# Second and third of four chained attentions: softmax sums beside PV, one reciprocal for eight heads, units in another order

## The chip, the core and the metric

One core of one Trainium2 chip runs the whole program. The metric is the device time of one execution in microseconds (us), from the host's start of the program to its end. TensorE is called PE here, VectorE DVE, ScalarE ACT, GpSimd POOL, and SyncE, which issues the transfers, SP.

## What is computed

Four cross-attentions in a chain, for 8 batches. Each takes the result of the one before as its queries (or latents) and a context of 256 columns or 128 rows as its keys. All have 16 heads. The second and third, which the change is about, are these (128 queries; 256 keys in the second, 128 in the third; 16 numbers per head):

```python
# second (L1): h = the context's 128 rows and then the 128 latents x
q  = (x @ q_w + q_b).reshape(b, 128, 16, 16)
k, v = split(h @ kv_w + kv_b)                  # 256 keys
attn = softmax(mask(q k^T / 16))
x1 = rmsnorm(attn v @ out_w + out_b + x, w)
x  = gelu(x1 @ mlp_w1 + mlp_b1) @ mlp_w2 + mlp_b2 + x

# third (L2): y = layer_norm(x), keys from the context's 128 rows
attn = softmax(mask(q k^T / 4))
h = attn v @ cproj_w + cproj_b + x
x = h + gelu(layer_norm(h) @ fc_w + fc_b) @ proj_w + proj_b
```

The first attention (L0) has 16 heads of 64 numbers with 256 queries and 256 keys, then an output projection and a layer norm. The fourth (L3) has 8 numbers per head, and takes the mean and the standard deviation of the values under the softmax.

## The kernel before

**Stages.** For each batch b the program works through L1, its MLP, L2, its MLP and L3. The L0 of batch b + 1 is laid between these pieces, and so are the projections of batch b + 1 (`qp0` to `qp3`, `kp0` to `kp3`, `vp0` to `vp3`: queries, keys and values), which fill gaps on PE. A last part, `mixed`, runs the second half of L0 for batch b + 1 and the whole of L3 for batch b step by step, in the order of the table `BOTH`. Batch 7 has no next batch, so L3 stands alone there (`LAST3`).

**Softmax in two passes.** For every group of heads a first pass in bf16 computes scores into the PSUM banks `MX` (a unit 0 or 2: two banks each), DVE takes their negated maxima with `tensor_reduce` (L1358) into `nm`, PE transposes these (a unit "T") and DVE copies them to `nmT` (L1345). The second pass computes the scores in f32 into the banks `SC`, with the maxima added by a matmul, and ACT takes the exponential into one of four slots of `Pr`. A group in L1 and L2 is 8 heads, in two halves of the partitions: two maxima units and a "T".

**PV in L1 and L2** (L886). The values of a head are 32 columns wide: 16 values and 16 ones. So one matmul gives the weighted values and, in the other 16 rows, the sum of the exponentials. Four heads (a quarter g) lie below each other in one PSUM bank. There are two PV banks, so the quarters g = 2 and 3 wait until DVE has finished g = 0 and 1. For each quarter DVE runs `quotient`: a gate instruction, a shuffle that lays the sums on the rows of the values (L1422), a reciprocal (L1423) and a product into `Ax` (L1424). The output projection `slots_out` (L948) has one matmul per quarter, four in all, since half of the rows are padding.

**What sets the order.** Nothing is scheduled at run time. Each engine works through its own list in the order of the code, with semaphores between the engines: `MX_SEQ` and `PV_SEQ` say which bank each use takes, in turns of two, and the outputs of projections take the two `GP` banks in turn, in the order of the list `BODY`. In L1 the order on PE is: maxima of group 0, transposed latents and the second value projection (`amid1`), `qp0`, "T", maxima of group 1 between the score steps, PV one step behind the scores, with `qp1`, `vp0` and the first maxima of the next L0 between. In L2 it is the same with `vp3` and one L0 unit, and then `k3` (L1046, keys of L3), the first two matmuls of the output, an L0 "T" with its scores, and the last two. DVE empties the `GP` banks of `qp0` to `qp3` into `Q0` (L1332); ACT empties those of `kp` and `vp`.

**Before L3** the three units `ENTRY` (first group's maxima and "T") run right ahead of L3's first scores, after L0's score step 4 and its PV.

Of the kernel before, what the change touches and what calls it, by code (L numbers as in the profile page):

```python
# [63 lines left out]
def alone(L):  # L64
# [14 lines left out]
LAST3[0][3].insert(0, (3, 1, 0))  # L79

# [5 lines left out]
def sequences():  # L86
# [9 lines left out]
    def mix(b, start, stop):  # L96
        for L, k, middle, end in mix_of(b)[start:stop]:
            if (L, k) == (3, 0):
                units(b, ENTRY)
# [11 lines left out]
    for b in range(B):  # L111
        more = b < B - 1
        banks0(b, [("xT",), ("lat",)] + [(1, g) for g in range(NG)])
# [6 lines left out]
        banks0(b, [(2, g) for g in range(NG)])  # L120
# [25 lines left out]
V_STEPS = 2 + 8 * 2 + 4  # L146
# [24 lines left out]
def build(nc, z_in, ctxT_in, ctx_in, mask1, mask2, mask3, w0, wo, w1qk, w1v, w1o, w1a, w1b,  # L171
          w2qkv, w2o, w2a, w2b, w3, cols_in, rows_in, ident_in, hmask_in, sel_in, out):
    with ExitStack() as stack:
# [21 lines left out]
        W1O = sb("W1O", [P, NG, D])  # L195
        W2QKV = sb("W2QKV", [P, 3, 2, D])
        W2O = sb("W2O", [P, NG, D])
# [10 lines left out]
        sums2 = sb("sums2", [P, 2, 32])  # L208
        stat0 = sb("stat0", [P, 20])
# [37 lines left out]
        V1 = sb("V1", [P, 2, NH, 32])  # L247
        K2 = sb("K2", [P, 2, P])
        K2b = sb("K2b", [P, 2, P], BF16)
        V2 = sb("V2", [P, NH, 32])  # L250
        K3 = sb("K3", [P, 2, D])
        K3b = sb("K3b", [P, 2, D], BF16)
        V3 = V1
        Ax = sb("Ax", [P, NG, P])
        junk3 = Ax[:, 0:2, :].rearrange("p g k -> p (g k)")
# [27 lines left out]
        scratch = nc.dram_tensor("scratch", [P, NG, D], F32, kind="Internal").ap()  # L283

# [106 lines left out]
        def pv_bank_taken(*use):  # L391
# [11 lines left out]
            return s_Ax, 8 * b + 4 * (kind - 1) + which[0] + 1  # L403
# [145 lines left out]
        def _(pe):  # L549
# [244 lines left out]
            def mixed(b, steps, make):  # L794
# [11 lines left out]
                for i in steps:  # L806
                    L, k, middle, end = mix[i]
                    if (L, k) == (3, 0):
                        for name in ENTRY:
                            unit(*name)  # L810
# [43 lines left out]
            def attention12(b, L, make, K, V, v_ready, amid=lambda: None, after=lambda i: None):  # L854
# [36 lines left out]
                entry, then = (UNITS1[:4], [UNITS1[4:5], UNITS1[5:]]) if L == 1 else (UNITS2[:3], [UNITS2[3:]])  # L891
                for _, g, u in entry:
                    if (g, u) == (0, "T"):
                        amid()
                    make(g, u)
                steps = [(c, kc) for c in range(2) for kc in range(halves)]
                for i, (c, kc) in enumerate(steps):
                    scores(c, kc)
                    if i == 1:
                        pe.wait_ge(*v_ready)  # L900
                    for _, g, u in (then[i] if i < len(then) else []):
# [9 lines left out]
            def body(b):  # L911
# [30 lines left out]
                def slots_out(name, W, which, between=None):  # L942
# [879 lines left out]
```

## Time and profile before

| | |
|---|---|
| median of 3 executions | 1221.82 us (1220.92 to 1226.72) |
| the profiled execution's own time | 1221.06 us |
| its span | 1219.3 us |
| PE busy | 991.2 us, 81% |
| DVE busy | 615.7 us, 50% |
| ACT busy | 463.1 us, 38% |
| POOL busy | 267.1 us, 22% |
| mean granted PE clock | 0.947 of full speed |

The span runs from the first to the last instruction, and the time of the execution lies 1.8 us above it. The first 71.8 us are the prologue (loads of the weights, projections and L0 of batch 0). From there on the batches follow each other at a nearly constant distance: the first DVE instruction of a batch (L1500) starts at 71.80, 212.85, 355.88, 499.25, 642.71, 785.99, 929.75 and 1072.68 us. The rows below are from the third of them, which is typical for the six in the middle. In a timeline row "[1.29 <-DVE Ax L1424]" means that the engine sat idle for 1.29 us before the row, and that the DVE instruction of line 1424, which writes `Ax`, released it. An f32 matmul shows as two records, so "x16" on L886 are 8 matmuls. PE works pipelined: the time from the start of one row to the start of the next says what a row costs in a stream, and the duration in the second column is longer.

### The profile page before, as it was taken

The page shows a single profiled execution, that of the slowest core. Times are in us where ns is not written, and L with a number is a line of the kernel's source. Part 1 is how long each engine was busy: PE and PEld are TensorE (multiplying, and loading weights), DVE is VectorE, ACT ScalarE, POOL GpSimd, SP SyncE. Part 2 cuts the span into 40 slices and gives each one's busy share as a digit, 9 for nine tenths or more (in the row PEclk, how much of TensorE's full clock was granted, in tenths as well). Part 3 has the DMA queues.
Part 4 walks back from the last instruction along what each step waited for, and adds up shares of the span by engine and source line. Part 5 has one row for each costly group of instructions (what it writes and reads, how often), then busy time and mean ns, then how long its engine had stood idle before and what let it go on. Part 6 is the DMA issues. An engine that isn't in the chain of part 4 may idle for free.

```text
span 1219.3 us, 20340 instructions
## 1 busy us (share of the span) xinstructions
PE 991.2 (81%) x7888; PEld 612.9 (50%) x7888; DVE 615.7 (50%) x1263; ACT 463.1 (38%) x881; POOL 267.1 (22%) x386
## 2 busy tenths in 40 slices
PE   7888789897897878888798878979788887976672
PEld 6465444564454654555546644546535454444430
DVE  1444544555546654465455555465544555554431
ACT  1414244343442444344342424424343344422223
POOL 0311111142111510232111421115112231023103
PEclk9899999999999999999999999999989999998667
DMA  9200120010200111002200102001020012001001
GB/s 379 93 1 1 70 95 26 6 70 5 96 31 1 74 51 55 22 2 74 95 19 14 66 10 95 31 2 74 9 87 31 2 74 86 17 16 69 5 1 35
DMA packets 29054, 60.60 MB, mean 50 GB/s; under 512 B 9376, under 2 KB 21024, under 8 KB 24096
## 3 DMA queue, kind: packets, MB, share of 16 engines
q1 hardware_dynamic: 28960, 59.29, 13.3%
q8 instruction: 65, 1.06, 0.4%
q14 instruction: 29, 0.24, 0.1%
HBM read 54.04 MB, written 5.24 MB: 49 GB/s over the span
## 4 chain that ended last, share of the span: by engine, by line
PE 68%; DVE 21%; issue 7%; ACT 2%; POOL 1%; DMA 1%; DVEq 0%; SPq 0%; POOLq 0%; ACTq 0%
DVE nm L1358 7%; PE GP L956 5%; PE PV L702 5%; PE GP L564 5%; PE GP L965 5%; PE GP L566 5%; DVE U L1423 5%; PE SC L685 3%; PE SC L771 3%; PE GP L938 3%; PE GP L749 3%; PE GP L788 3%; PE SC L873 2%; PE MX L618 2%; PE GP L948 2%
## 5 line engine op out<-in xcount | busy, mean ns | idle before, releaser
L1358 DVE TENSOR_REDUCE nm<-MX 128x2 bf16<-128x512 f32 (+1 forms) x352 | 227.1, 689 | 203.1 <-PE MX L624 111.5
L1672 POOL TENSOR_TENSOR Psum<-Pr 128x512 f32<-128x512 f32 x56 | 70.9, 1266 | 294.4 <-ACT Pr L1164 294.4
L1166 ACT ACTIVATE Pr<-SC,bcol 128x512 f32<-128x512 f32 x128 | 81.1, 684 | 131.5 <-PE SC L771 131.5
L564 PE MATMUL GP<-zP,W 128*128 128x128 f32 x512 | 103.2, 284 | 6.9 <-DMA W<-w 6.9
L1191 ACT ACTIVATE Pr<-SC,bcol 128x512 f32<-128x512 f32 x96 | 60.8, 684 | 115.8 <-PE SC L873 115.8
L566 PE MATMUL GP<-uP,W 128*128 128x128 f32 x512 | 100.1, 277 | 0.0
L1164 ACT ACTIVATE Pr<-SC 128x512 f32<-128x512 f32 x128 | 69.3, 593 | 62.8 <-PE SC L685 62.8
L564 PEld LDWEIGHTS GP<-zP,W 128*128 128x128 f32 x512 | 79.8, 194 | 15.8 <-issue 13.6
L1646 POOL TENSOR_TENSOR stat<-stat,half 128x1 f32<-128x1 f32 x24 | 13.6, 565 | 326.9 <-DVE stat L1532 179.2
L566 PEld LDWEIGHTS GP<-uP,W 128*128 128x128 f32 x512 | 78.9, 195 | 0.0
L702 PE MATMUL PV<-Pr,V 128*64 128x256 f32 x512 | 75.6, 420 | 0.0
L965 PE MATMUL GP<-WB,work 128*128 128x256 f32 x256 | 62.2, 398 | 10.5 <-DVE work L1461 10.5
L771 PE MATMUL SC<-work,K 64*128 64x512 f32 x256 | 70.3, 619 | 0.0
L685 PE MATMUL SC<-Q,K 64*128 64x256 f32 x512 | 70.2, 384 | 0.0
L956 PE MATMUL GP<-oT,WA 128*128 128x128 f32 x512 | 65.2, 289 | 0.9 <-issue 0.8
L956 PEld LDWEIGHTS GP<-oT,WA 128*128 128x128 f32 x512 | 62.4, 203 | 4.8 <-issue 3.5
L886 PE MATMUL PV<-Pr,V 128*32 128x128 f32 x768 | 35.8, 290 | 33.0 <-DVE Ax L1424 32.0
L1423 DVE RECIPROCAL U<-U 128x128 f32<-128x128 f32 x64 | 61.0, 953 | 2.2
L965 PEld LDWEIGHTS GP<-WB,work 128*128 128x128 f32 x256 | 49.4, 198 | 23.2 <-issue 16.5
L1345 DVE COPY nmT<-MX 128x256 bf16<-128x256 bf16 (+1 forms) x96 | 25.7, 267 | 59.4 <-PE MX L657 47.6
L873 PE MATMUL SC<-work,K 64*128 64x512 f32 x192 | 54.8, 638 | 0.0
L685 PEld LDWEIGHTS SC<-Q,K 64*128 64x128 f32 x512 | 51.4, 192 | 4.1
(184 smaller groups left out, 1709.0 us busy)
## 6 DMA issues: line engine op xcount, KB each, us to landing
WA<-w1a SPq DMA_DIRECT2D x8, 1024.0 KB, 6.0
WB<-w1b SPq DMA_DIRECT2D x8, 1024.0 KB, 8.1
WA<-w2a SPq DMA_DIRECT2D x8, 1024.0 KB, 5.0
WB<-w2b SPq DMA_DIRECT2D x8, 1024.0 KB, 7.1
W<-w SPq DMA_DIRECT2D x6, 1024.0 KB, 9.9
scratch<-U SPq DMA_DIRECT2D x16, 256.0 KB, 2.0
C<-scratch SPq DMA_DIRECT2D x96, 32.0 KB
zP<-z_in SPq DMA_DIRECT2D x8, 128.0 KB, 4.3
```

Of the source, the lines that this page charges most:

```text
L564: pe.matmul(dst, W0[:, piece, 2 * s, at:at + P], zP[:, s * P:s * P + P], start=True, stop=False)
L566: mm = pe.matmul(dst, W0[:, piece, 2 * s + 1, at:at + P], uP[:, s * P:s * P + P], start=False, stop=True)
L685: mm = pe.matmul(SC[r][:, kc * D:kc * D + D], K0[half, k, kc * P:kc * P + P], Q0[half, k, :], start=False, stop=True, skip_group_check=True)
L702: mm = pe.matmul(bank[64 * j:64 * j + 64, i * D:i * D + D], V0[:, kc, h * 64:h * 64 + 64], Pr[:, (n + j) % 4, kc * D:kc * D + D], start=(k ...
L771: pe.matmul(SC[j][:].rearrange("p (t l) -> p t l", l=D), K3[half, g % 2, kc * P:kc * P + P], Q3[half, g // 2 * 2:g // 2 * 2 + 2, :], start ...
L873: pe.matmul(SC[r][:].rearrange("p (t l) -> p t l", l=P), K[half, c, kc * P:kc * P + P], Q12[half, 4 * c:4 * c + 4, :], start=False, stop=True,
L956: mm = pe.matmul(g[:, j * P:j * P + P], WA[:, c, f * P:f * P + P], oT[:, c, :], start=(c == 0), stop=(c == 1), skip_group_check=True)
L965: mm = pe.matmul(g[:, 0:D], G[:, f * P:f * P + P], WB[:, f, :], start=(f == 0), stop=(f == 7))
L1166: act.activation(Pr[:, (n + j) % 4, :], SC[j], ACT.Exp, bias=bcol[:, 3 + k % 2:4 + k % 2], scale=8.0 ** -0.5).then_inc(p_ready, 1)
L1358: dve.tensor_reduce(dst, MX[(n + i) % 2][:].rearrange("p (a k) -> p a k", a=a), AX_X, ALU.max, negate=True).then_inc(mx_done, 1)
L1423: chain.step(dve.reciprocal(den, den))
L1672: pool.tensor_tensor(Psum[:, c % 4, :].rearrange("p (a l) -> p a l", l=D), two[:, :, 0:D], two[:, :, D:2 * D], ALU.add)\
```

## The change

It has four parts.

1. **Sums beside PV.** The values are now laid out so that the 32 columns of a head hold 16 values in the lower half for one quarter and in the upper half for the other, with zeros in the rest. Both quarters of a group accumulate into one bank, columns 0 to 127. A second set of matmuls with a small tile of ones (`ones2`) as weights puts the sums at the same rows, columns 128 to 255. `quotient` then needs no shuffle and runs once for 8 heads, twice in a layer in place of four times, with its reciprocal straight from PSUM. `slots_out` has two matmuls. V3 becomes a tile of its own.
2. **Steps in another order in L1 and L2.** The latents' transposes and the second value projection follow the first maxima unit, `qp0` the second; `vp0` moves behind PV; `k3` moves between the score steps of L2; the L0 "T" stands between the two PV steps, and its scores ahead of the two output matmuls.
3. **The entry of L3.** In batches 0 to 6 the three units that begin L3 are spread over L0's score steps 4 and 5 (`BOTH`); step 5 of L0 comes ahead of L3's first scores. The reciprocal of L0's first sums (`reciprocals0`) keeps its place behind the "T" of L3's second group.
4. **Query projections.** `qp0` to `qp3` of the next batch are emptied by ACT, two activations of 256 columns each with a bias, in place of one DVE instruction of 512.

```diff
@@ order of steps, all engines
-        (0, 4, [], []), (3, 0, [], [(3, 1, 0)]), (3, 1, [], [(3, 1, 2)]), (0, 5, [(3, 1, "T")], [(0, 3, 0)]),
-        (3, 2, [], [(0, 3, 2)]), (3, 3, [(0, 3, "T")], [(3, 2, 0)]), (0, 6, [], [(3, 2, 2)]),
+        (0, 4, [(3, 0, 0)], [(3, 0, 2)]), (0, 5, [(3, 0, "T")], [(3, 1, 0)]), (3, 0, [], [(3, 1, 2)]),
+        (3, 1, [(3, 1, "T")], [(0, 3, 0)]), (3, 2, [], [(0, 3, 2)]), (3, 3, [(0, 3, "T")], [(3, 2, 0)]),
...
+def entry(b):
+    return ENTRY if b == B - 1 else []
@@ PE, PV of L1 and L2
                     for r in range(2):
-                        g = 2 * c + r
-                        bank = pv_bank(b, L, g)
                         pe.wait_ge(p_ready, n + r + 1)
-                        if kc == 0:
-                            pe.wait_ge(*pv_bank_taken(b, L, g))
-                        for t in range(4):
-                            mm = pe.matmul(bank[32 * t:32 * t + 32, 0:P], V(HG * g + t, kc),
-                                           Pr[:, (n + r) % 4, t * P:t * P + P], start=(kc == 0),
-                                           stop=(kc == halves - 1), skip_group_check=True)
+                        for at, weights in ((0, lambda t: V(2 * c + r, t, kc)), (P, lambda t: ones2[:, r, :])):
+                            for t in range(4):
+                                mm = pe.matmul(bank[32 * t:32 * t + 32, at:at + P], weights(t),
+                                               Pr[:, (n + r) % 4, t * P:t * P + P], start=(at == kc == r == 0),
+                                               stop=(kc == halves - 1 and r == 1), skip_group_check=True)
@@ PE, slots_out
-                    for s in range(NG):
-                        if s == 2 and between:
-                            between()
-                        pe.wait_ge(s_Ax, 8 * b + 4 * which + s + 1)
+                    for s in range(2):
+                        pe.wait_ge(s_Ax, 4 * b + 2 * which + s + 1)
@@ PE, L1
-                def amid1():
+                def amid1(g, u):
+                    if (g, u) == (0, 0):
...
+                        v1("v1c", 0)
+                    if (g, u) == (0, 2):
+                        fill("qp0")
...
-                    if i in (1, 2):
-                        fill("qp1" if i == 1 else "vp0")
+                    if i == 1:
+                        fill("qp1")
...
+                fill("vp0")
                 slots_out("o1", W1O, 0)
@@ PE, L2
+                def before2(i):
+                    if i == 0:
+                        g, full = begin("k3", (ld_w3, 16))
...
                 def after2(i):
-                    if more and i == 0:
-                        make03[0](1, 2)
+                    if more:
+                        make03[0](1, "T" if i else 2)
...
-                def between2():
-                    if more:
-                        make03[0](1, "T")
-                        scores0(b + 1, 2)
-                slots_out("o2", W2O, 1, between2)
+                if more:
+                    scores0(b + 1, 2)
+                slots_out("o2", W2O, 1)
@@ ACT
+                if name[0] == "q":
+                    for c in range(2):
+                        ins = act.activation(Q0[:, 2 * i + c, :], g[:, c * D:c * D + D], ACT.Identity,
+                                             bias=col("rwb", 2 * i + c))
+                    ins.then_inc(s_Q0, 1)
...
-                attention12(b, 1, 1.0 / 16, lambda i: cast(b + 1, 0) if more and i == 3 else None)
+                fill("qp0")
+
+                def after1(i):
+                    if more and i == 3:
+                        fill("qp1")
+                        cast(b + 1, 0)
+                attention12(b, 1, 1.0 / 16, after1)
...
-                fill("vp2", "vp3")
-                attention12(b, 2, 0.25)
-                g = take(o, "k3")
+                fill("qp2", "vp2", "vp3")
+
+                def keys3(i):
+                    if i != 1:
+                        return
+                    g = take(o, "k3")
...
+                attention12(b, 2, 0.25, keys3)
...
+                fill("qp3")
                 turned("yT2", "ln2w", "ln2b")
@@ DVE
-                    if L == 0 and k == 5:
+                    if (L, k) == ((0, 5) if b < 0 else (3, 1)) and b < B - 1:
                         reciprocals0(b + 1, 0)
...
-            def quotient(b, L, g):
+            def quotient(b, L, m):
...
-                chain.step(dve.stream_shuffle(den, bank, [16 + r % 16 for r in range(32)]))
-                chain.step(dve.reciprocal(den, den))
-                dve.tensor_tensor(Ax[:, g, :], bank, den, ALU.mult).then_inc(s_Ax, 1)
+                chain.step(dve.reciprocal(den, bank[:, P:2 * P]))
+                dve.tensor_tensor(Ax[:, m, :], bank[:, 0:P], den, ALU.mult).then_inc(s_Ax, 1)
```

**PE, end of L2, before**: L886 is PV (all four quarters), L1046 is `k3`, L948 the output, L657 the L0 "T", L679 and L685 its scores.

```order
L660 MATMUL MX<-identb,nm 128x128
L603 MATMUL MX<-K0b,Qb 128x256 x4
L869 MATMUL SC<-nmT,sel 128x128 x8
L873 MATMUL SC<-work,K 128x512 x2
L886 MATMUL PV<-Pr,V 32x128 x16
L1046 MATMUL GP<-uC,W 128x256
L948 MATMUL GP<-W2O,Ax 128x256 x2
L657 MATMUL MX<-identb,nm 128x128 x2
L679 MATMUL SC<-nmT,sel 128x512 x2
L685 MATMUL SC<-Q,K 128x256 x4
L948 MATMUL GP<-W2O,Ax 128x256 x2
L702 MATMUL PV<-Pr,V 64x256 x4
```

The same place after; L897 is PV with its sums, L667 the L0 "T", L689 and L695 its scores, L958 the output.

```order
L897 MATMUL PV<-Pr,V 32x128 x4
L897 MATMUL PV<-Pr,ones 32x128 x4
L897 MATMUL PV<-Pr,V 32x128 x4
L897 MATMUL PV<-Pr,ones 32x128 x4
L667 MATMUL MX<-identb,nm 128x128 x2
L897 MATMUL PV<-Pr,V 32x128 x4
L897 MATMUL PV<-Pr,ones 32x128 x4
L897 MATMUL PV<-Pr,V 32x128 x4
L897 MATMUL PV<-Pr,ones 32x128 x4
L689 MATMUL SC<-nmT,sel 128x512 x2
L695 MATMUL SC<-Q,K 128x256 x4
L958 MATMUL GP<-W2O,Ax 128x256 x2
```

PV has twice the matmuls, the L0 "T" has moved between its two steps, the output's two matmuls stand together behind L0's scores, and `k3` has gone forward (it now stands between the two score steps, ahead of these rows).

**PE, where L3 begins, before**: L679 and L685 are L0's score step 4, L702 its PV, L723 its sums, L618 and L624 the maxima of L3, L657 their "T", L767 and L771 L3's first scores.

```order
L679 MATMUL SC<-nmT,sel 128x512 x2
L685 MATMUL SC<-Q,K 128x256 x4
L702 MATMUL PV<-Pr,V 64x256 x4
L723 MATMUL PV<-Psum,sums 32x256 x4
L618 MATMUL MX<-b3row,sel 128x512 x2
L624 MATMUL MX<-K3b,Q3b 128x256 x4
L618 MATMUL MX<-b3row,sel 128x512 x2
L624 MATMUL MX<-K3b,Q3b 128x256 x4
L657 MATMUL MX<-identb,nm 128x128 x2
L767 MATMUL SC<-nmT,sel 128x256 x4
L771 MATMUL SC<-work,K 128x512 x2
L702 MATMUL PV<-Pr,V 64x256 x4
```

And after, where every line number is 10 higher:

```order
L689 MATMUL SC<-nmT,sel 128x512 x2
L695 MATMUL SC<-Q,K 128x256 x4
L628 MATMUL MX<-b3row,sel 128x512 x2
L634 MATMUL MX<-K3b,Q3b 128x256 x4
L712 MATMUL PV<-Pr,V 64x256 x4
L733 MATMUL PV<-Psum,sums 32x256 x4
L628 MATMUL MX<-b3row,sel 128x512 x2
L634 MATMUL MX<-K3b,Q3b 128x256 x4
L689 MATMUL SC<-nmT,sel 128x512 x2
L695 MATMUL SC<-Q,K 128x256 x4
L667 MATMUL MX<-identb,nm 128x128 x2
L712 MATMUL PV<-Pr,V 64x256 x4
```

Between the first maxima unit and the second now stand PV and sums of L0, and between the second and the "T" L0's score step 5.

**DVE, end of L1, before** (L425 is the gate, L1529 takes the output) and, in the second fence, after (L435 the gate, L1451 and L1452 the quotient, L1393 maxima of the next L0, L1557 takes the output):

```order
L1423 RECIPROCAL U<-U 128x128
L1424 TENSOR_TENSOR Ax<-PV,U 128x128
L1358 TENSOR_REDUCE nm<-MX 128x2 x2
L425 TENSOR_TENSOR gate<-half 128x1
L1422 STREAM_SHUFFLE U<-PV 128x128
L1423 RECIPROCAL U<-U 128x128
L1424 TENSOR_TENSOR Ax<-PV,U 128x128
L425 TENSOR_TENSOR gate<-half 128x1
L1422 STREAM_SHUFFLE U<-PV 128x128
L1423 RECIPROCAL U<-U 128x128
L1424 TENSOR_TENSOR Ax<-PV,U 128x128
L1529 TENSOR_TENSOR xa<-GP,res 128x256
```

```order
L435 TENSOR_TENSOR gate<-half 128x1
L1451 RECIPROCAL U<-PV 128x128
L1452 TENSOR_TENSOR Ax<-PV,U 128x128
L1393 TENSOR_REDUCE nm<-MX 128x2 x4
L435 TENSOR_TENSOR gate<-half 128x1
L1451 RECIPROCAL U<-PV 128x128
L1452 TENSOR_TENSOR Ax<-PV,U 128x128
L1557 TENSOR_TENSOR xa<-GP,res 128x256
```

Four quotients have become two, without shuffles, and both maxima units of the next L0 stand between them.

## Rows read from the trace of the kernel before

**Rows 1.** The page's first part: busy time, share of the span, instructions.
```profile
PE 991.2 (81%) x7888; PEld 612.9 (50%) x7888; DVE 615.7 (50%) x1263; ACT 463.1 (38%) x881; POOL 267.1 (22%) x386
```

**Rows 2.** Waits over the span: waiter, releaser, us in total, times, longest.
```profile
PE PV L886 <- DVE Ax L1424: 32.0, 23, 2.1
...
PE GP L948 <- DVE Ax L1424: 27.4, 30, 1.8
```

**Rows 3.** Windows of batch 2: length, busy times (instructions), granted PE clock, DMA share, GB/s.
```profile
355.90:499.20 143.30, 121.21 (x988) 74.78 (x987) 76.88 (x157) 57.63 (x110) 33.42 (x47) 0.98 0.12 43
419.00:435.40 16.40, 10.72 (x93) 5.89 (x93) 9.44 (x26) 5.82 (x11) 2.39 (x4) 0.90 0.03 10
461.70:480.00 18.30, 17.41 (x152) 8.36 (x152) 9.99 (x16) 8.76 (x15) 2.54 (x2) 0.91 0.05 15
```

**Rows 4.** Timeline of PE in L1: start, duration, line, instruction, idle before and releaser.
```profile
367.14 0.39 PE L638 MATMUL MX<-b1row,sel 64*128 64x512 bf16 x2 [1.56 <-DVE nm L1358]
...
371.77 0.39 PE L638 MATMUL MX<-b1row,sel 64*128 64x512 bf16 x2 [0.95 <-DVE nmT L1345]
...
376.26 0.69 PE L886 MATMUL PV<-Pr,V 128*32 128x128 f32 x16
...
376.88 0.49 PE L564 MATMUL GP<-zP,W 128*128 128x128 f32 x2
...
385.88 0.42 PE L886 MATMUL PV<-Pr,V 128*32 128x128 f32 x8 [1.29 <-DVE Ax L1424]
...
389.71 0.70 PE L948 MATMUL GP<-W1O,Ax 128*128 128x256 f32 x2 [1.45 <-DVE Ax L1424]
391.31 0.70 PE L948 MATMUL GP<-W1O,Ax 128*128 128x256 f32 x2 [0.91 <-DVE Ax L1424]
391.85 0.28 PE L657 MATMUL MX<-identb,nm 128*128 128x128 bf16 x2
```

**Rows 5.** Timeline of PE in L2, to the transposes behind it.
```profile
421.78 0.40 PE L603 MATMUL MX<-K0b,Qb 64*128 64x256 bf16 x4 [0.41 <-DVE nmT L1345]
...
423.31 0.64 PE L886 MATMUL PV<-Pr,V 128*32 128x128 f32 x16
425.70 0.43 PE L886 MATMUL PV<-Pr,V 128*32 128x128 f32 x8 [1.75 <-DVE Ax L1424]
...
431.33 0.39 PE L679 MATMUL SC<-nmT,sel 64*128 64x512 bf16 x2 [0.39 <-DVE nmT L1345]
...
432.93 0.70 PE L948 MATMUL GP<-W2O,Ax 128*128 128x256 f32 x2 [0.35 <-DVE Ax L1424]
...
435.45 1.08 PE L702 MATMUL PV<-Pr,V 128*64 128x256 f32 x8
...
439.78 0.41 PE L930 MATMUL GP<-ident,xb 128*128 128x128 f32 x2 [1.27 <-DVE xb L1472]
```

**Rows 6.** Timeline of PE where L3 begins.
```profile
457.67 0.39 PE L618 MATMUL MX<-b3row,sel 64*128 64x512 bf16 x2 [1.58 <-DVE nm L1358]
...
459.84 0.27 PE L657 MATMUL MX<-identb,nm 128*128 128x128 bf16 x2 [1.56 <-DVE nm L1358]
...
461.71 1.97 PE L702 MATMUL PV<-Pr,V 128*64 128x256 f32 x8
```

**Rows 7.** Groups of instructions: busy us, mean ns of one, idle before them.
```profile
L1358 DVE TENSOR_REDUCE nm<-MX 128x2 bf16<-128x512 f32 x320 | 206.5, 690 | 189.7 <-PE MX L624 111.5 <-PE MX L603 54.0 <-PE MX L644 24.2
...
L1423 DVE RECIPROCAL U<-U 128x128 f32<-128x128 f32 x64 | 61.0, 953 | 2.2
L1191 ACT ACTIVATE Pr<-SC,bcol 128x512 f32<-128x512 f32 x96 | 60.8, 684 | 115.8 <-PE SC L873 115.8
...
L1404 DVE RECIPROCAL xb<-PV 128x256 f32<-128x256 f32 x16 | 28.0, 1753 | 2.3 <-PE PV L720 1.2 <-DVE work L1412 0.5
...
L1424 DVE TENSOR_TENSOR Ax<-PV,U 128x128 f32<-128x128 f32 x64 | 18.7, 292 | 2.2
...
L1256 ACT ACTIVATE K1b<-GP,cols 128x256 bf16<-128x256 f32 x16 | 6.7, 472 | 25.0 <-PE GP L938 25.0
```

More of the change, by code:

```diff
@@ L112, in sequences @@
         more = b < B - 1
-        banks0(b, [("xT",), ("lat",)] + [(1, g) for g in range(NG)])
+        banks0(b, [("xT",), ("lat",), (1, 0), (1, 1)])
         units(b, UNITS1)
@@ L119, in sequences @@
             banks0(b + 1, [("pv", 0)])
-        banks0(b, [(2, g) for g in range(NG)])
+        banks0(b, [(2, 0), (2, 1)])
         units(b, UNITS2)
@@ L808, in mixed @@
                     if (L, k) == (3, 0):
-                        for name in ENTRY:
+                        for name in entry(b):
                             unit(*name)
@@ L852, in mix_end, with attention12 @@
                     project("kp0", order_of(b + 1), b + 2)
[L854 removed]
+            def attention12(b, L, make, K, V, v_ready, amid=lambda g, u: None, before=lambda i: None,
+                            after=lambda i: None):
                 halves = 2 if L == 1 else 1
@@ L898, in attention12 @@
                     scores(c, kc)
+                    before(i)
                     if i == 1:
                         pe.wait_ge(*v_ready)
-                    for _, g, u in (then[i] if i < len(then) else []):
+                    for _, g, u in (units[cuts[i]:cuts[i + 1]] if i + 1 < len(cuts) else []):
                         make(g, u)
@@ L1320, in _ @@
             chain = Chain(dve, v_step, V_STEPS)
-            apart = Apart(dve, gate[:, 1:2], v_apart, 11)
+            apart = Apart(dve, gate[:, 1:2], v_apart, 7)
             def take(o, name):
@@ L1372, in mixed @@
                     if (L, k) == (3, 0):
-                        for name in ENTRY:
+                        for name in entry(b):
                             unit(*name)
@@ L1386, in mix_end, with attention12 @@
                     quotient0(b + 1, 3)
-            def attention12(b, L, amid=lambda: None, after=lambda: None, during=lambda g: None):
-                units = UNITS1 if L == 1 else UNITS2
-                for _, g, u in units:
-                    if (g, u) == (0, "T"):
-                        amid()
+            def attention12(b, L, amid=lambda g, u: None):
+                for _, g, u in UNITS1 if L == 1 else UNITS2:
                     maxima(b, L, g, u)
-                after()
-                for g in range(NG):
-                    quotient(b, L, g)
-                    during(g)
+                    amid(g, u)
             def reciprocals0(b, half):
@@ L1519, in body, with amid1 @@
                 more = not is_last(b)
-                def after1():
-                    fill("qp1")
-                    if not is_first(b):
-                        end3(b - 1)
-                attention12(b, 1, lambda: (v1("v1c", 0), fill("qp0")), after1,
-                            lambda g: maxima(b + 1, 0, 0, 2 * g) if more and g < 2 else None)
+                def amid1(g, u):
+                    if (g, u) == (0, 0):
+                        v1("v1c", 0)
+                attention12(b, 1, amid1)
+                if not is_first(b):
+                    end3(b - 1)
+                quotient(b, 1, 0)
+                if more:
+                    maxima(b + 1, 0, 0, 0)
+                    maxima(b + 1, 0, 0, 2)
+                quotient(b, 1, 1)
                 g = take(o, "o1")
@@ L1549, in body @@
                     maxima(b + 1, 0, 1, 0)
-                fill("qp2")
                 blocks12(b, o, 2)
-                attention12(b, 2, after=lambda: maxima(b + 1, 0, 1, 2) if more else None,
-                            during=lambda g: maxima(b + 1, 0, 1, "T") if more and g == 1 else None)
+                attention12(b, 2)
+                if more:
+                    maxima(b + 1, 0, 1, 2)
+                quotient(b, 2, 0)
+                if more:
+                    maxima(b + 1, 0, 1, "T")
+                quotient(b, 2, 1)
                 g = take(o, "o2")
```

123 lines of the change are left out of this document (65 added, 58 removed), and 4 rows, old and new, of the table BOTH.

## The prediction

> **What bounds the kernel now.** I read the page first: PE is busy for 991 of 1219 us, and no other engine for more than 616 [rows 1]. So PE sets the pace, and the question is only how much of its idle and slow time the change removes and how much work it adds. The list of waits comes next. Two of PE's longest have one releaser, the product at the end of a quotient: 32.0 us before PV of L1 and L2, which wants its bank back, and 27.4 us before the output projections [rows 2]. A window over one batch gives the budget: 143.3 us with PE busy for 121.2 [rows 3], which leaves 22.1 us idle. The clock is a second loss. Over two stretches of that batch it is granted at 0.90 and 0.91 [rows 3], which means 1.2 GHz for 3.3 us of each and 2.4 GHz for the rest, some 1.65 us lost in each. The timelines of PE show where the waits lie; they repeat in all middle batches. I work out one batch, and multiply by 7. The last batch has no work of a next batch to move.
>
> **First attention of the pair (L1).** At its start PE waits 1.56 us for the first maxima and 0.95 us for the copy of their transpose [rows 4], 2.51 in all. The latents' transposes and the second value projection move into the first of these. At 0.54 us per f32 matmul of 256 columns (391.31 to 391.85, [rows 4]) they fill about 1.15 us of it, and 0.4 stay. The copy no longer queues behind the emptying of qp0 on DVE; the wait for such a copy with nothing in front is 0.41 [rows 5]. Gain 2.51 - 0.4 - 0.4 = 1.7 us.
>
> At its end three waits for `Ax` go: 1.29, 1.45 and 0.91 [rows 4], 3.65 us. A wait costs PE more than its idle figure, since the pipeline empties first: I take 0.15 us for each, 0.45. Two of four output matmuls go, 1.08. Against this stands what PV gains in work. 16 records of PV take 0.62 us from their start to that of the next row (376.26 to 376.88, [rows 4]), and a call now has 32. The trace has no call with sums beside it. The least is 0, if the sums ran alongside in other columns; the most is 0.245 us for each of 16 records, a pair of full matmuls being 0.49 [rows 4], 3.9 us. I take the row that is nearest, the same form with the same shapes: 0.62 us more for each call, 2.5 for four.
>
> What is late next is ACT: it now empties qp1 (two activations at 0.47, [rows 7]) and makes the two casts for the next L0 before the third pair of exponentials (2 x 0.68), while vp0, which covered that, has moved back. I charge 0.6 us of wait, with 0 and 1.5 as ends. The last quotient has gate, reciprocal 0.95 and product 0.29 [rows 7]. The reciprocal now reads PSUM; the trace has this form only at twice the width, 1.75 us [rows 7], so it costs between 0.95 and 1.75, and I take 0.95, nearly all of its time being per element (1.75 is less than twice 0.95). It starts behind the reduces of the next L0's second unit (2 x 0.69, [rows 7]), and is done about 1.8 us after PV; vp0 covers that. Gain 3.65 + 0.45 + 1.08 - 2.5 - 0.6 = 2.1 us.
>
> **Second attention (L2).** From the L0 unit at 421.78 to the PV of L0 at 435.45 it takes 13.7 us now [rows 5]. I walk through what follows. k3 moves ahead of the "T"; it takes about 1.0 us and covers a wait of 0.4, so the L0 unit starts 0.6 later, and PV at 423.9 in place of 423.31. PV 1.24, the L0 "T" 0.15, PV 1.24: 426.5. None of the two waits for a quotient, since each has a bank of its own. DVE can begin the first quotient at 425.1: gate 0.15, 0.95, 0.29, then the copy of the "T", about as long as the product, with hops 0.2: 427.0, so that L0's scores wait 0.5. They take 1.25 us (431.33 to 432.93 less the wait of 0.35, [rows 5]): 428.35. The second quotient is ready at 428.4. Two output matmuls: 429.4. Gain 435.45 - 429.4 = 6.05 us; it is the largest term, as waits of 1.75, 0.41, 0.39 and 0.35 us ([rows 5], and others between those rows) and the slow clock of this stretch lie in it.
>
> Behind it the transposes of xb come 4.33 us after the output (435.45 to 439.78, [rows 5]), with a wait of 1.27 that the emptying of qp3 on DVE helped to cause. PV of L0 and qp3 need 2.9, plus 0.3 for exponentials that are now late: gain 1.1. But ACT empties qp3 first (0.94) and oT after it, and that holds the MLP up by 0.55. Gain 0.55. In front of L2, qp2 on ACT costs 0.1.
>
> **Entry of L3.** Two waits of 1.58 and 1.56 [rows 6] go with 0.3 for the pipeline, 3.45 us: L0's PV, sums and scores now stand where PE waited for the reduces. What follows at half clock (8 records of L0's PV in 1.97 us, [rows 6], against 1.08, [rows 5]) returns to full speed, 1.65. New waits: a unit's reduces take 1.38 [rows 7] plus two hops, and the work between is a little shorter in three places, 0.15 + 0.35 + 0.35. The move of L0's first reciprocal on DVE (1.75) stays behind the same "T". Gain 4.25 us.
>
> **At nothing:** the four DVE projections that go (DVE is idle half of the time), memsets in the prologue, where all wait for weights, and V3's own tile. SP issues the same transfers in the same order, and none lies in a gap above.
>
> **Sum.** 1.7 + 2.1 + 6.05 + 0.55 - 0.1 + 4.25 = 14.55 us per batch, 101.9 for seven. In the last batch nothing can be moved into the gaps, ACT bounds L1 and the entry of L3 is unchanged; I give it 3 us, a fifth of the others. Together 104.9, against the profiled execution's own 1221.06 us: 1116 us. The median is 0.8 above that execution, within the noise. As a check, a batch would take 128.8 us with PE busy for 121.2 + 6 x 0.62 - 4 x 0.54 - 3.3 = 119.5, 93%.
>
> **Rivals.** (1) The clock stays down in both stretches. For it: the new order still has five short waits there. Against it: every fall in the timeline follows a group of waits that are gone. Price 3.3 x 7 = 23 us: 1139 us. The Trainium skill, "TensorE: Matmul & The Clock Gate", section "A second HAM failure mode: psum-queue depth-cycling", speaks for it: a PE that idles briefly between groups often enough has its clock swing between the levels. Rows show both levels near waits, not which length of wait decides. (2) ACT becomes what PE waits for. Four emptyings of 0.94 stand in its queue ahead of exponentials, casts or oT. I charge 0.6 + 0.55 + 0.1; if all 3.76 come on the path, 2.5 x 7 = 18 us: 1134 us. Against it: ACT is idle in more than half of the batch. (3) The new order hides nothing, as its waits come back one step later: 1.7 + 4.25 less per batch, 42 us: 1158 us. Against it: the work moved in is longer than each wait but three. (4) The slower side: the ones do not run four abreast like the values, but one after another at 0.245 us each. That is 3.3 us more per call, 48 calls, 158 us: 1274 us. It decides from 105 / 48 = 2.2 us over my 0.62, or 0.18 us a record. Against it: values with the same shape take 0.039 us each (0.62 / 16).
>
> **Chances.** Forecast, 1100 to 1130 by itself: 0.62. Rival 1: 0.13. Rival 2: 0.12. Rival 3: 0.07. Rival 4: 0.03. The sums run for nothing (-30 us, 1086): 0.03. The range 1092 to 1150 holds the first three. A measurement can tell 0.5%, 6 us, from no change: faster 0.96, within 0.01, slower 0.03.
>
> **What would show it.** Batches 127 to 131 us apart. No wait of PV in L1 and L2 for DVE, and at most 0.6 us before the output of L2. The call of PV at 1.2 to 1.3 us from start to start: over 2 shows rival 4. Full clock between L2's PV and its output, and at the start of L3: else rival 1. The wait of L1's fourth score step for ACT near 0.6, and the MLP's first matmul about 0.5 later against the transposes: if over 1, rival 2. If the first maxima of L3 still have waits over 1 us behind them, rival 3. The forecast is wrong if the batches are more than 135 us apart.

## The result, and the profile after

The changed kernel takes 1095.26 us (median of 4 runs, 1094.25 to 1096.86) against 1223.36 us for the kernel before, run beside it: a ratio of 0.895, 95% interval 0.893 to 0.898. I had predicted 1116 us, with a range of 1092 to 1150. The direction and the mechanism held; 127.2 us of span went where I had counted 104.9. The page's first line, against [rows 1]:

```profile
PE 955.9 (88%) x8592; PEld 608.2 (56%) x8592; DVE 541.6 (50%) x1012; ACT 484.3 (44%) x937; POOL 268.1 (25%) x389
```

PE is busy for only 35 us less, so most of the gain is idle time. Windows over the third batch (323.44 to the next start), the end of L2 and the entry of L3, with columns as in [rows 3]:

```profile
323.44:449.98 126.54, 117.28 (x1076) 74.77 (x1075) 67.17 (x125) 60.68 (x118) 33.49 (x47) 1.00 0.14 49
381.00:391.30 10.30, 8.98 (x124) 5.25 (x122) 5.79 (x14) 4.94 (x9) 3.16 (x6) 1.00 0.04 14
415.00:433.00 18.00, 16.28 (x158) 7.49 (x154) 10.87 (x18) 7.72 (x13) 1.95 (x2) 1.00 0.10 23
```

A batch takes 126.5 us instead of 143.3, PE's idle time in it falls from 22.1 to 9.3 us, and the clock is full in both stretches that ran at 0.90 and 0.91. The waits on `Ax` of [rows 2], 27.4 and 32.0 us, have shrunk to this, and none of them is before PV any more:

```profile
PE GP L958 <- DVE Ax L1452: 2.1, 3, 0.9
```

To place the gain I read four starts on DVE in each batch: the sum `x0` (batch start), the two sums `xa` behind the outputs of L1 and L2, and `x3` behind the second MLP. The distances in the third batch, in us, with those of the experiments below (the last batch runs from its `x0` to the end of the span):

| kernel | x0 to xa of L1 | to xa of L2 | to x3 | to next x0 | batch | last batch |
|---|---|---|---|---|---|---|
| before | 36.17 | 43.50 | 15.99 | 47.71 | 143.37 | 146.62 |
| changed | 31.45 | 36.57 | 15.22 | 43.33 | 126.57 | 135.43 |
| e1 old entry of L3 | 31.45 | 36.58 | 15.21 | 48.68 | 131.92 | 136.06 |
| e2 queries on DVE | 31.70 | 36.42 | 16.09 | 43.33 | 127.54 | 136.56 |
| e3 old order in L1, L2 | 33.44 | 37.27 | 15.57 | 43.33 | 129.61 | 136.41 |
| e4 layout only | 33.98 | 37.13 | 16.45 | 48.73 | 136.29 | 140.16 |
| e5 ones three times | 32.75 | 37.00 | 15.22 | 43.33 | 128.30 | 138.12 |
| e6 reciprocal twice | 32.78 | 38.21 | 15.03 | 43.33 | 129.35 | 140.77 |
| e7 e1, waits filled | 31.44 | 36.58 | 15.22 | 46.13 | 129.37 | 137.18 |
| e8 last batch filled | 31.45 | 36.58 | 15.21 | 43.34 | 126.58 | 125.13 |
| e9 before, filled | 36.12 | 41.81 | 15.99 | 46.13 | 140.05 | 130.30 |

At full clock the sections repeat to 0.05 us between kernels that do not differ in them, and from batch to batch but for the first and the fifth, so terms of 0.2 us can be read. Where the clock falls they do not repeat. In the kernel before, L2's section takes 42.63 to 43.50 us over the seven full batches, and the third has the longest; in e1 the entry of L3 takes 47.51 to 48.90. So where the clock is in play I give the mean of the seven batches too. From before to changed the means are 4.64, 6.61, 0.78 and 4.46 us, and in the third batch 4.72, 6.93, 0.77 and 4.38. The total cannot be read finely: the start of the first batch moves between 71 and 74 us, in part because the first matmul waits 6.9 to 8.3 us for its weights. One of the four executions of e1 took 2639.64 us; without it the median of e1 is 1129.9 instead of 1130.3.

PE in the changed kernel from the first PV of L2, against [rows 5]:

```profile
386.30 0.43 PE L897 MATMUL PV<-Pr,V 128*32 128x128 f32 x8
386.54 0.40 PE L897 MATMUL PV<-Pr,ones 128*32 128x128 f32 x8
386.76 0.40 PE L897 MATMUL PV<-Pr,V 128*32 128x128 f32 x8
386.98 0.40 PE L897 MATMUL PV<-Pr,ones 128*32 128x128 f32 x8
387.31 0.29 PE L667 MATMUL MX<-identb,nm 128*128 128x128 bf16 x2
387.53 0.43 PE L897 MATMUL PV<-Pr,V 128*32 128x128 f32 x8
...
389.11 0.39 PE L689 MATMUL SC<-nmT,sel 64*128 64x512 bf16 x2 [0.50 <-DVE nmT L1380]
389.34 1.03 PE L695 MATMUL SC<-Q,K 64*128 64x256 f32 x8
390.29 1.13 PE L958 MATMUL GP<-W2O,Ax 128*128 128x256 f32 x4
391.54 1.08 PE L712 MATMUL PV<-Pr,V 128*64 128x256 f32 x8
```

Where PV waited 1.75 us, the "T" and the other PV call now follow without a wait. The one wait left is the 0.50 us that I had expected. The call takes 1.01 us (386.30 to 387.31), not 1.24. And the entry of L3, against [rows 6]:

```profile
413.37 0.27 PE L667 MATMUL MX<-identb,nm 128*128 128x128 bf16 x2 [0.49 <-DVE nm L1393]
413.58 1.08 PE L712 MATMUL PV<-Pr,V 128*64 128x256 f32 x8
...
419.41 0.27 PE L667 MATMUL MX<-identb,nm 128*128 128x128 bf16 x2 [0.50 <-DVE nm L1393]
...
422.97 0.39 PE L613 MATMUL MX<-K0b,Qb 64*128 64x256 bf16 x4 [0.74 <-DVE nm L1393]
```

The eight records of L0's PV take 1.08 us again, where they took 1.97.

### The profile page after: what moved, and what is told of

It is laid out like the page before. It is cut to its first block, busy times and chain, and to the rows that moved or that the text cites. A ratio compares the mean times of both kernels' runs of the same rounds, so it can differ in the third digit from the quotient of the medians.

```text
span 1092.1 us, 21492 instructions
## 1 busy us (share of the span) xinstructions
PE 955.9 (88%) x8592; PEld 608.2 (56%) x8592; DVE 541.6 (50%) x1012; ACT 484.3 (44%) x937; POOL 268.1 (25%) x389
## 4 chain that ended last, share of the span: by engine, by line
PE 72%; DVE 12%; issue 9%; ACT 4%; POOL 1%; DMA 1%; DVEq 0%; ACTq 0%; POOLq 0%; SPq 0%
DVE nm L1393 6%; PE PV L712 6%; PE GP L966 6%; PE GP L574 6%; PE GP L975 5%; PE GP L576 5%; PE SC L695 4%; PE GP L950 4%; PE SC L884 3%; PE GP L759 3%; PE SC L781 3%; PE GP L798 2%; PE GP L581 2%; PE PV L897 2%; PE MX L628 2%
## 5 line engine op out<-in xcount | busy, mean ns | idle before, releaser
L1393 DVE TENSOR_REDUCE nm<-MX 128x2 bf16<-128x512 f32 (+1 forms) x352 | 227.0, 689 | 169.7 <-PE MX L634 79.6
L712 PE MATMUL PV<-Pr,V 128*64 128x256 f32 x512 | 69.4, 392 | 0.8
L695 PE MATMUL SC<-Q,K 64*128 64x256 f32 x512 | 68.6, 382 | 0.0
L975 PE MATMUL GP<-WB,work 128*128 128x256 f32 x256 | 59.3, 384 | 10.5 <-DVE work L1489 10.5
L781 PE MATMUL SC<-work,K 64*128 64x512 f32 x256 | 67.7, 598 | 0.0
L884 PE MATMUL SC<-work,K 64*128 64x512 f32 x192 | 55.0, 637 | 0.0
L695 PEld LDWEIGHTS SC<-Q,K 64*128 64x128 f32 x512 | 50.9, 190 | 4.3
L1671 POOL TENSOR_TENSOR work<-qs,hmask 128x512 f32<-128x512 f32 x32 | 32.6, 1041 | 82.9 <-DVE Q12b L1467 82.9
L1128 ACT ACTIVATE K<-GP 128x512 f32<-128x512 f32 x32 | 19.1, 597 | 76.0 <-PE GP L576 76.0
L1477 DVE TENSOR_TENSOR work<-GP,cols 128x512 f32<-128x512 f32 x32 | 22.1, 691 | 61.1 <-PE GP L966 61.1
```

The costliest lines, as they stand in the source:

```text
L695: mm = pe.matmul(SC[r][:, kc * D:kc * D + D], K0[half, k, kc * P:kc * P + P], Q0[half, k, :], start=False, stop=True, skip_group_check=True)
L712: mm = pe.matmul(bank[64 * j:64 * j + 64, i * D:i * D + D], V0[:, kc, h * 64:h * 64 + 64], Pr[:, (n + j) % 4, kc * D:kc * D + D], start=(k ...
L781: pe.matmul(SC[j][:].rearrange("p (t l) -> p t l", l=D), K3[half, g % 2, kc * P:kc * P + P], Q3[half, g // 2 * 2:g // 2 * 2 + 2, :], start ...
L884: pe.matmul(SC[r][:].rearrange("p (t l) -> p t l", l=P), K[half, c, kc * P:kc * P + P], Q12[half, 4 * c:4 * c + 4, :], start=False, stop=True,
L975: mm = pe.matmul(g[:, 0:D], G[:, f * P:f * P + P], WB[:, f, :], start=(f == 0), stop=(f == 7))
L1393: dve.tensor_reduce(dst, MX[(n + i) % 2][:].rearrange("p (a k) -> p a k", a=a), AX_X, ALU.max, negate=True).then_inc(mx_done, 1)
```

## The experiments

**e1: the old entry of L3.**

```diff
 def entry(b):
-    return ENTRY if b == B - 1 else []
+    return ENTRY
 # and BOTH, with the place of reciprocals0, as before
```

> The changed kernel with the entry of L3 as before: the three units of maxima in one row ahead of L3's first scores, and the order of the mixed part of L0 and L3 with the place of L0's first reciprocal as before. All else as changed. My theory, by the section from x3 to the next batch's start (47.71 us before, 43.33 after): two waits of about 1.6 us on the reduces and about 1.65 us of half clock come back in each of 7 batches, 4.4 x 7 = 31 us: 1126 us, and a granted clock of about 0.9 at the entry. Rival A: only the waits count and the clock stays at 2.4 GHz since the stretches ahead are denser: 2.7 x 7 = 19 us, 1114 us. Rival B: the section became shorter for another reason (Q3 or the MLP): within 5 us of the changed kernel.

1130.3 us (0.9226 of before, interval 0.9203 to 0.9249). My theory holds: only the last section changes, by 5.35 us in the third batch and 4.82 in the mean of seven, where the change had gained 4.38 and 4.46. The order and the waits are again those of before, but in this batch PE runs at half clock for longer, from the scores at 426.37 on:

```profile
425.61 0.37 PE L667 MATMUL MX<-identb,nm 128*128 128x128 bf16 x2 [1.56 <-DVE nm L1393]
426.37 0.60 PE L777 MATMUL SC<-nmT,sel 64*128 64x256 bf16 x4 [0.39 <-DVE nmT L1380]
426.77 1.91 PE L781 MATMUL SC<-work,K 64*128 64x512 f32 x4
428.61 1.97 PE L712 MATMUL PV<-Pr,V 128*64 128x256 f32 x8
430.52 0.61 PE L628 MATMUL MX<-b3row,sel 64*128 64x512 bf16 x2
```

The matmuls at L781 take 1.91 us here; at full clock they take 1.02 (e7, below).

It is not so in every batch. Windows over 18 us from `x3` on, of the third and the fourth batch:

```profile
417.31:435.31 18.00, 13.94 (x98) 5.99 (x96) 7.08 (x13) 6.92 (x14) 1.99 (x2) 0.81 0.46 160
549.24:567.24 18.00, 13.86 (x114) 6.20 (x114) 7.79 (x15) 7.93 (x15) 2.01 (x3) 0.91 0.46 160
```

Both have the waits of 1.58 and 1.56 us, but the second of them has half the time at 1.2 GHz. The section takes 48.5 to 48.9 us in the first, third, fifth and seventh batch, and 47.5 to 47.6 in the three others.

**e2: queries back on DVE.** `project("qp0")` to `("qp3")` are emptied by one DVE operation each, where they were before.

> The changed kernel with the emptying of the four query projections back on DVE, one operation each, at the places that they had before. My theory: ACT's part costs 1.25 us per batch by the prediction (0.6 + 0.55 + 0.1), and on DVE the copy of the first transpose and xb wait longer again, 0.95 + 0.5 us: the two nearly cancel, 0 to +5 us, 1095 to 1100 us. Rival A: ACT's emptyings are what PE now waits for, and the kernel is faster by up to 1.25 x 7 = 9 us, 1086 us. Rival B: DVE's queue was the true cause of the old waits in L1 and L2: slower by over 15 us.

1102.7 us (0.9005, 0.8985 to 0.9025). Emptying by ACT in place of DVE is a gain of about 1 us per batch (0.97 in the third), and the kernel is 2.7 us above my bound of 1100. The table puts 0.87 of it behind L2, where `xb` waits again:

```profile
395.36 1.08 PE L712 MATMUL PV<-Pr,V 128*64 128x256 f32 x8
...
399.62 0.41 PE L942 MATMUL GP<-ident,xb 128*128 128x128 f32 x2 [1.20 <-DVE xb L1497]
```

That is 4.26 us from L0's PV to the transposes, against 2.94 in the changed kernel (391.54 to 394.48). Rival A, a kernel that is faster without the emptyings on ACT, is refuted.

**e3: the old order within L1 and L2**, on the new layout.

```diff
-                    if i == 1:
-                        fill("qp1")
+                    if i in (1, 2):
+                        fill("qp1" if i == 1 else "vp0")
 # latents, v1c and qp0 behind (0, 2); k3 behind L2; the "T" and
 # scores0(b + 1, 2) between the two output matmuls of L2
```

> The changed kernel with PE's order within L1 and L2 as before: latents' transposes, v1c and qp0 after the second unit, vp0 inside L1's steps instead of ahead of the output, k3 after L2, and the 'T' and the scores of L0 between the two matmuls of L2's output. Layout, entry of L3 and the emptying by ACT stay. My theory, from the terms: 1.15 us at L1's start, about 0.9 us that vp0 covers ahead of L1's output, and of L2's 6 us some 1.5 to 2 (0.5 that k3 covered, a wait for the second quotient partly covered, and some half clock): about 3.8 x 7 = 27 us, 1122 us. Rival A: the layout alone made the gain, and the order is worth under 1 us per batch: below 1102 us. Rival B: the orders carry the clock too: over 40 us, above 1135 us.

1121.5 us (0.9161, 0.9135 to 0.9187), as expected, but in part by luck. The order is worth 1.99 us in L1, where I had 2.05, but 0.70 in L2, where I had 1.5 to 2, and 0.35 behind it. Those 3.04 us make 21 in seven batches; the rest is a first batch that starts 1.5 us later and costs 1.7 us more than the others, and a last one that costs 1.0. Without `vp0` to cover it, the second quotient is what L1's output waits for:

```profile
365.44 0.70 PE L960 MATMUL GP<-W1O,Ax 128*128 128x256 f32 x2 [1.10 <-DVE Ax L1451]
```

**e4: the layout only**, with e1, e2 and e3 undone together.

> Of the change only the layout: sums beside PV in columns of their own, one reciprocal for eight heads, two output matmuls. The entry of L3, PE's orders in L1 and L2 and the emptying by DVE are as before. My theory: the parts add, and the layout is the largest, 128 - 31 - 27 - 3 = 67 us of the gain: 1095 + 61 = 1156 us. Rival A: with the old orders the waits on the second quotient come back in place of those on the bank, and the layout alone gives only half of that: about 1190 us. Rival B: the layout is nearly all of it: below 1130 us.

1171.3 us (0.9557, 0.9528 to 0.9587), between my theory and rival A: the layout alone brings 53 of the 128 us. By section the parts nearly add: this kernel's batch is 9.72 us longer than the changed one's, and e1 to e3 give 5.35 + 0.97 + 3.04 = 9.36. Over seven batches it is 67.2 against 63.1 us; 3.3 of these 4.1 us lie at the entry of L3, where this kernel has the long stretch at half clock in six batches and e1 in four. I had undershot since I had put the three parts too low (61 us for 35, 7.5 and 26 measured), and the last batch adds 4.7 us. The layout alone brings 6.37 of L2's 6.93 us (6.05 of 6.61 in the mean), the clock included. From its window over the section between the two `xa`:

```profile
376.34:413.47 37.13, 34.89 (x290) 23.27 (x288) 20.00 (x39) 18.58 (x36) 17.67 (x27) 1.00 0.17 62
```

**e5: the price of a pass beside PV.**

```diff
-                        for at, weights in ((0, ...), (P, lambda t: ones2[:, r, :])):
+                        for at, weights in ((0, ...), (P, lambda t: ones2[:, r, :]),
+                                            (2 * P, lambda t: ones2[:, r, :])):
```

> The changed kernel with a third pass in each PV call of L1 and L2: 8 more matmuls of the ones for each half, into the unused columns 256 to 383 of the bank. What is computed stays the same. This measures the price of a pass that runs beside PV, 16 records per call, 48 calls. My theory, from the timeline of the changed kernel (a call with sums takes 1.02 us, one without took 0.62): 0.40 x 48 = 19 us, 1114 us. Rival A, the prediction's term: 0.62 x 48 = 30 us, 1125 us. Rival B: the pass is hidden where PE waits anyway for the exponentials: below 5 us, under 1100 us.

1110.4 us (0.9082, 0.9062 to 0.9102). Sixteen records more per call cost 0.44 us where nothing hides them:

```profile
347.65 0.43 PE L898 MATMUL PV<-Pr,V 128*32 128x128 f32 x8
347.89 0.62 PE L898 MATMUL PV<-Pr,ones 128*32 128x128 f32 x16
348.33 0.40 PE L898 MATMUL PV<-Pr,V 128*32 128x128 f32 x8
```

Each 8 records take 0.22 us from start to start (347.89 to 348.33 is 0.44 for 16). Of 6 x 0.44 = 2.64 us per batch 1.73 reach the end: 1.30 of the 1.76 us of L1's four calls, and 0.43 of the 0.88 of L2's two. The rest falls into waits. Both the term of the prediction, 0.62, and rival B are refuted.

**e6: the reciprocal of each quotient twice.**

```diff
-                chain.step(dve.reciprocal(den, bank[:, P:2 * P]))
+                for _ in range(2):
+                    chain.step(dve.reciprocal(den, bank[:, P:2 * P]))
 # and V_STEPS, the count of chained DVE steps, 2 + 8 + 4 in place of 2 + 4 + 4
```

> The changed kernel with the reciprocal of each quotient taken twice, the second one overwriting the first with the same numbers: 32 more DVE instructions of about 0.95 us, each waiting for the one before. My theory: at the ends of L1 and L2 the DVE chain is on the path although DVE is idle half of the time. In L2 the first quotient stands ahead of the copy of L0's 'T' and the second ahead of the output, where PE waits 0.41 and 0.50 us now: 2 x 1.05 us. In L1 vp0 covers about 0.5 of 1.05. That makes 2.6 x 7 = 18 us and 4 us in the last batch: 1117 us. Rival: DVE's idle time takes it up: under 5 us, below 1100 us.

1120.6 us (0.9162, 0.9140 to 0.9185): 2.78 us per batch, 2.6 expected, and 5.3 in the last. DVE is idle half of the time, yet its chain at the ends of L1 and L2 is on the path: the wait ahead of L0's scores is 1.49 where it was 0.50.

```profile
399.47 0.39 PE L689 MATMUL SC<-nmT,sel 64*128 64x512 bf16 x2 [1.49 <-DVE nmT L1380]
```

**e7: e1 with PE busy in the two waits at the entry of L3.** A helper issues n matmuls on constants into unused columns of the bank that is taken next:

```diff
+            def warm(b, name, n):
+                o = order_of(b)
+                pe.wait_ge(*o.bank_taken(name))
+                for _ in range(n):
+                    pe.matmul(GP[o.at(name)[0]][:, D:2 * D].rearrange("p (a k) -> p a k", k=P), identb[:],
+                              sel[:, 0:2, :], start=True, stop=True, skip_group_check=True)
```

> The kernel with the old entry of L3 (the one that measured 1130.3 us), with 10 bf16 matmuls of 256 columns on constants, into unused columns of the bank that u0 takes next, behind each of the two units of maxima that PE waits for there. They fill the two waits of 1.58 and 1.56 us and give nothing else. My theory: the section's 5.35 us over the changed kernel are 2.7 us of waits and 2.65 us of half clock (5.3 us at 1.2 GHz); with PE busy in the waits the clock stays at 2.4 GHz and only the waits are left: 1130.3 - 2.65 x 7 = 1112 us. Rival A: the clock falls by something else than these idle stretches, and the time stays at 1130 us or rises. Rival B: waits and clock are one loss and all of it comes back: 1095 us.

1117.5 us (0.9141, 0.9121 to 0.9160). The section falls from 48.68 to 46.13. So 2.55 us of e1's 5.35 are clock and 2.80 waits, as expected for this batch. In the mean of the seven, e1's 4.82 are 2.01 of clock and 2.81 of waits, since three batches of e1 had the short stretch. The total is 5.5 us above my number. In the profiled executions the clock gives back 14.1 us and not the 18.6 that I had multiplied out, the first batch starts 1.7 us later (74.1 us), and the last one is 1.1 us longer. The same stretch:

```profile
421.92 1.27 PE L591 MATMUL GP<-sel,identb 128*128 128x256 bf16 x10
423.55 0.27 PE L675 MATMUL MX<-identb,nm 128*128 128x128 bf16 x2 [0.36 <-DVE nm L1403]
424.21 0.39 PE L785 MATMUL SC<-nmT,sel 64*128 64x256 bf16 x4 [0.39 <-DVE nmT L1390]
424.44 1.02 PE L789 MATMUL SC<-work,K 64*128 64x512 f32 x4
```

**e8: the changed kernel with its last batch filled.** One `warm` of 3 to 24 matmuls in most long waits of the last batch, as `if not more: warm(b, "yT", 24)` ahead of the transposes of `xb`.

> The changed kernel, with PE kept busy in the last batch: behind most of its waits of over 0.5 us stand 3 to 24 bf16 matmuls of 256 columns on constants, into unused columns of the bank that is taken next, sized to be a little shorter than the wait. My theory: the last batch runs a third of its time at 1.2 GHz (granted 0.83, 0.82, 0.89, 0.77 by section), and PE's own work there lies on the path, so some 8 us come back: 1087 us, with a granted clock of 0.95 or more in the last batch. Rival A: the chain of DVE, ACT and POOL sets the last batch's time, and the clock gives under 2 us. Rival B: the fillers delay the work behind them, since they take longer than the waits: slower than 1095 us.

1085.6 us (0.8879, 0.8861 to 0.8898): the fastest version here. The last batch falls from 135.4 to 125.1 us. The windows over it, of the changed kernel and then of e8:

```profile
956.67:1092.10 135.43, 79.51 (x662) 48.34 (x662) 50.52 (x101) 41.48 (x78) 30.85 (x51) 0.81 0.07 26
```

```profile
956.97:1082.10 125.13, 92.09 (x877) 60.97 (x877) 51.54 (x101) 41.56 (x78) 31.00 (x51) 0.93 0.08 29
```

PE has 215 more matmul records and yet the batch ends 10.3 us sooner: its own work runs at 2.4 GHz to its end. The granted clock is 1.00 until 1065.2 us, and PE's last matmul ends at 1061.6.

**e9: the kernel before with its waits filled**, by the same helper.

> The kernel before, with bf16 matmuls of 256 columns on constants in its longest waits, and nothing else changed: in every batch 12 and 8 of them ahead of the third and fourth quarter of L2's PV, 8 ahead of the last output matmul of L2, 11 and 11 behind the first two units at the entry of L3; in the last batch also in the waits of the kernel whose last batch was filled before. It parts the clock from the waits. My theory: in the two stretches that ran at 0.90 and 0.91, 1.65 us each come back and the waits stay: 3.3 x 7 = 23 us; the last batch (146.6 us) keeps its waits on the quotients but loses its half clock: with the changed kernel's filled last batch at 125.1 us it ends at 129 us, 17 us less. Together 1223 - 40 = 1183 us. So of the change's 11.2 us in the last batch some 7 would be the clock. Rival A: the clock is not held by such filling while the waits are this long: above 1210 us. Rival B: the clock sets most of L2's gain: L2's section falls by 3 us or more from its 43.5, below 1170 us.

1188.6 us (0.9704, 0.9678 to 0.9731), 5.6 above my theory, which holds against both rivals. In the third batch L2's section loses 1.69 us and the last one 1.58: the half clock of [rows 3] and nothing else. At the entry of L3 the clock stays full in all seven batches (1.69 us in the mean). Ahead of it it does not: four batches still have some half clock in L1 or L2. The fourth has it in both, here from `x0` to the first `xa` and on to the second:

```profile
493.85:530.83 36.98, 30.14 (x268) 20.62 (x266) 21.84 (x53) 10.33 (x19) 4.18 (x5) 0.96 0.02 6
530.83:573.75 42.92, 40.51 (x292) 26.62 (x292) 22.95 (x52) 19.90 (x38) 17.07 (x27) 0.95 0.14 53
```

So L2 gives back 1.22 us in the mean, L1 loses 0.44, and the seven batches give 17.3 us where I had 23, which is about what was missing. In the last batch 16.3 us come back:

```profile
1056.90:1187.20 130.30, 94.29 (x806) 61.33 (x806) 58.90 (x129) 41.71 (x78) 31.07 (x51) 0.93 0.08 28
```

At equal clock the last batches differ by 130.30 - 125.13 = 5.2 us.

## Why the prediction held, and which terms were off

**L1: 3.8 forecast, 4.72 measured.** The waits went as said, and ACT's new one is 0.35 us, not 0.6:

```profile
348.43 0.39 PE L880 MATMUL SC<-nmT,sel 64*128 64x128 bf16 x7 [0.35 <-ACT Pr L1215]
```

The mis-sized term is the PV call: I charged 0.62 us for the sums, since 16 records stood 0.62 us from the next row in [rows 4]. Those 0.62 hold something that a call pays once: in the changed kernel each 8 records take 0.22 us, and a call of 32 takes 1.01. The extra is 0.40, and e5 gives 0.44 for the next 16. Four calls at 0.22 us less are 0.9, of which 0.65 would reach the end by the share that e5 measured in L1. With ACT's 0.25 the sum comes to 4.7 to 4.9, against 4.72.

**L2: 5.95 forecast (6.05 less the 0.1 of `qp2`), 6.93 measured.** Two calls explain up to 0.44 more. `k3`, charged at 1.0 us from a stretch at half clock, takes 0.54 (383.65 to 384.19), another 0.46:

```profile
383.65 0.70 PE L1061 MATMUL GP<-uC,W 128*128 128x256 f32 x2
384.19 0.22 PE L670 MATMUL MX<-identb,nm 128*128 128x128 bf16 x1
```

With both my walk gives 6.85. (One of its steps is added up wrong: 427.0 + 1.25 is 428.25 and not 428.35, which moves the end by 0.1 us at most.) e9 shows that 1.69 of the term is clock in this batch, as I had read from the granted 0.90 (1.22 in the mean), and e4 that the layout, not the order, brings nearly all of it. e6 shows that the DVE chain still sets this end.

**Behind L2: 0.55 forecast, 0.77 measured.** The transposes come 1.32 us sooner with `qp3` off DVE (2.94 in place of 4.26), and the MLP's first matmul 0.44 later behind them (1.80 us in place of 1.36): 0.88 against e2, and against my 1.1 - 0.55.

```profile
394.48 0.41 PE L942 MATMUL GP<-ident,xb 128*128 128x128 f32 x2
...
395.53 0.71 PE L1080 MATMUL GP<-W,uC 128*128 128x128 f32 x4 [0.32 <-ACT Q L1124]
396.28 3.81 PE L966 MATMUL GP<-oT,WA 128*128 128x128 f32 x32
```

**Entry of L3: 4.25 forecast, 4.38 measured.** The waits are worth 2.80 (46.13 less 43.33, both at full clock), where I had 3.45 - 0.85 = 2.6. The clock is worth 1.58, where I had 1.65.

**Last batch: 3 forecast, 11.2 measured.** This is the step that failed by most. I said that nothing could be moved there, and scaled the waits. But both last batches have long stretches at half clock, and the change shortens those too: e8 and e9 leave 5.2 us of waits and work, so 6.0 us were clock. The profile of the kernel before shows it in a window over that batch, with a granted clock of 0.76, which my term leaves out:

```profile
1072.68:1219.30 146.62, 86.26 (x574) 51.90 (x574) 57.91 (x129) 41.60 (x78) 30.41 (x51) 0.76 0.07 24
```

Together: the seven full batches gained 115.4 us against 101.9 (of the 13.5 over, the PV calls are at most 6 x 0.22 x 7 = 9.2 and `k3` 3.2), the last one 8.2 more than said, the start of the first batch 0.65. The misses do not cancel, they add: every section of the third batch gained more than forecast, and 126.6 us from batch to batch lies just under the 127 to 131 that I had named. The measured 1095 us is inside the range, but 3 us from its lower end and below the 1100 to 1130 to which I had given 0.62. The other signs came as said: no wait of PV for DVE in L1 and L2, full clock in both stretches, no wait over 1 us at the entry of L3.

**The rivals.** (1) The clock stays down: no; it is 1.00 through the middle batches, with waits of 0.3 to 0.9 us left. The Trainium skill, "TensorE: Matmul & The Clock Gate", section "A second HAM failure mode: psum-queue depth-cycling", spoke for it: it tells of a PE whose short idles between groups of matmuls make the clock swing. This trace does not bear that out for its short waits, behind which the clock is 1.00. Behind two waits of about 1.6 us at the entry of L3 it fell in all seven batches of e1, and with them filled it stayed at 1.00 in all seven (e7). (2) ACT as the bound: no (e2). (3) Waits that only move: no, except for 0.49, 0.50 and 0.74 us at the entry. (4) Ones one after another: no, 0.027 us a record (e5).

## What to carry over

A wait of PE costs its idle time and then, behind some groups of long ones, half clock in the work that follows. The rows do not say which groups: the two of 1.6 us at the entry of L3 did it in every batch, while the three of 1.29, 1.45 and 0.91 us at the end of L1 [rows 4] stand in a window of the kernel before with the full clock:

```profile
384.00:396.00 12.00, 7.88 (x65) 4.03 (x63) 7.15 (x22) 3.49 (x9) 2.24 (x8) 1.00 0.01 1
```

Read the granted clock over every stretch and in every batch, the last one too, and price the two apart: constant matmuls in the waits do it in one run (not in every batch of e9), and where the waits cannot go they are worth keeping (e8). Do not multiply one batch's loss by seven before you have seen that it repeats. A short burst of records timed to the next row holds a cost that a longer burst pays only once; take the price of more records from the distance between rows inside a burst. An engine that is idle half of the time can still end the path, so lengthen its chain once to see.

## What the runs showed that I had not expected

The same waits in the same order cost a different amount of clock, and this in one and the same kernel. Behind 1.58 and 1.56 us at the entry of L3 the section of e1 is longer than that of e7, which has the full clock, by 1.4 us in three batches and by 2.4 to 2.6 in four. The kernel before has the small loss in six batches, 1.58 us in the third (e9), and the large one in the sixth, where the section takes 48.45 us and not 47.7; e4 has the small loss in its first batch (47.78) and the large one in the others. The sixth batch of the kernel before, in a window of 18 us from `x3` on, has the 0.81 of e1's third:

```profile
881.30:899.30 18.00, 13.86 (x100) 6.00 (x98) 7.09 (x13) 7.15 (x14) 1.99 (x2) 0.81 0.47 161
```

So the layout by itself does not make this section slower: with the small loss it takes 47.5 us in e1 and 47.7 in the kernel before. What decides between the short and the long stretch, and whether the layout makes the long one more frequent, is open.

The reciprocal that reads PSUM takes no longer than the one that read SBUF, 949 against 953 ns [rows 7], as I had assumed:

```profile
L1451 DVE RECIPROCAL U<-PV 128x128 f32<-128x128 f32 x32 | 30.4, 949 | 0.0
```
